# Two gated cross-attention and feed-forward layers: all five engine streams in another order, with the same operations

## The reference

```python
x = x + tanh(g_xattn[0]) * L0_xattn(ctx, ctx, layernorm(x), Wk, Wq, Wv, Wo, biases)   # A
x = x + tanh(g_ffn[0])   * L0_ffn(layernorm(x), w_gate, w_up, w_down)                 # B
x = x + tanh(g_xattn[1]) * L1_xattn(layernorm(x), ctx, Wq, Wkv, Wo)                   # C
x = x + tanh(g_ffn[1])   * L1_ffn(layernorm(x), W, b, lora_down, lora_up, ...)        # D

# A: 16 heads of width 16, the softmax is over the heads
score = einsum('bhij,bhkj->bhik', k, q) / sqrt(16);  attn = softmax(score, axis=1)
# B: h = silu(x @ wg.T) * (x @ wu.T), 768 wide; h @ wd.T
# C: 16 query heads, one key and value head of width 16, softmax over the context rows
# D: a linear layer whose weight has a low-rank addition
```

## Time and profile before

| | |
|---|---|
| median of 3 executions | 2359.47 us (2358.21 to 2359.94) |
| profiled execution | 2358.72 us, its span 2356.9 us |
| mean granted clock of PE | 0.999 of full speed |
| busy share of the span | PE 98%, DVE 93%, POOL 75%, ACT 72% |
| busy share of the 16 DMA engines | 9.9% |
| period of the loop | 35.24 us, 57 iterations |

### The profile page before, as it was taken

How to read it: one execution, slowest core, us unless ns; L and a number is a source line. 1 busy time by engine, 2 the same in 40 slices (tenths; PEclk the granted TensorE clock), 3 DMA queues, 4 the chain that set the end, 5 groups by cost and what they waited for, 6 DMA issues and landing times.

```text
span 2356.9 us, 69621 instructions
## 1 busy us (share of the span) xinstructions
PE 2308.5 (98%) x27827; PEld 2062.3 (87%) x27827; DVE 2200.9 (93%) x3613; ACT 1705.6 (72%) x3402; POOL 1777.8 (75%) x2512
## 2 busy tenths in 40 slices
PE   6999999999999999999999999999999999999998
PEld 5888888889888888888889889889889889889887
DVE  6999999999999999999999999999999999999973
ACT  4667777777777777777777777777777777777664
POOL 3767787787787787787787777777778778778754
PEclk9999999999999999999999999999999999999999
DMA  3000010010010010010010100100100100000000
GB/s 110 28 22 28 29 34 27 29 34 27 29 34 27 29 34 27 29 34 27 31 33 27 34 29 27 34 29 27 34 29 28 33 29 30 31 29 32 20 22 15
DMA packets 74332, 73.33 MB, mean 31 GB/s; under 512 B 6555, under 2 KB 73393, under 8 KB 74290
## 3 DMA queue, kind: packets, MB, share of 16 engines
q1 hardware_dynamic: 74290, 72.75, 9.9%
HBM read 54.90 MB, written 16.78 MB: 30 GB/s over the span
## 4 chain that ended last, share of the span: by engine, by line
PE 56%; DVE 37%; issue 3%; ACT 1%; POOL 1%; DMA 1%; SPq 0%; POOLq 0%; DVEq 0%; ACTq 0%
DVE m L1600 11%; PE work L2383 10%; PE work L2384 9%; PE work L2385 9%; PE scores L2480 6%; PE work L2513 5%; PE work L2500 5%; DVE scores L1597 5%; DVE m L1591 4%; PE work L2420 4%; PE scores L2470 4%; DVE x L1628 4%; PE work L2398 2%; DVE stats_B L1559 2%; DVE stats_D L1559 2%
## 5 line engine op out<-in xcount | busy, mean ns | idle before, releaser
L856 ACT ACTIVATE e<-scores 120x1024 f32<-120x1024 f32 x512 | 517.5, 1042 | 35.9 <-DVE scores L1597 21.5
L2383 PE MATMUL work<-xt_hi_B,w_hi 128*128 128x256 f32 x1536 | 445.0, 290 | 2.8 <-POOL xt_lo_B L426 2.8
L2384 PE MATMUL work<-xt_lo_B,w_hi 128*128 128x256 f32 x1536 | 426.9, 278 | 0.0
L2385 PE MATMUL work<-xt_hi_B,w_lo 128*128 128x256 f32 x1536 | 426.6, 278 | 0.0
L413 POOL TENSOR_TENSOR zt<-e 120x512 f32<-120x512 f32 x256 | 331.1, 1295 | 49.5 <-ACT e L856 40.9
L407 POOL TENSOR_TENSOR h_lo<-h_f,h_hi 128x256 fp32r<-128x256 f32 x384 | 278.9, 740 | 90.5 <-ACT h_hi L803 90.4
L1597 DVE TENSOR_TENSOR scores<-scores,m 120x1024 f32<-120x1024 f32 x256 | 303.0, 1227 | 4.2
L2383 PEld LDWEIGHTS work<-xt_hi_B,w_hi 128*128 128x128 f32 x1536 | 290.8, 189 | 17.0 <-POOL xt_lo_B L426 13.5
L1609 DVE TENSOR_TENSOR e<-e,work 120x2048 f32<-120x2048 f32 x128 | 291.4, 2276 | 0.2
L1591 DVE TENSOR_REDUCE m<-scores 120x128 fp32r<-120x2048 f32 x128 | 290.0, 2266 | 0.9 <-PE scores L2470 0.8
L2384 PEld LDWEIGHTS work<-xt_lo_B,w_hi 128*128 128x128 f32 x1536 | 289.3, 188 | 0.0
(11 more groups left out here) (224 smaller groups left out, 7290.6 us busy)
## 6 DMA issues: line engine op xcount, KB each, us to landing
x_ln<-xp SPq DMA_DIRECT2D x64, 256.0 KB, 2.9
x_res<-xp SPq DMA_DIRECT2D x64, 256.0 KB, 2.8
y<-y_out SPq DMA_DIRECT2D x64, 256.0 KB, 2.2
ctx_f_A<-cp SPq DMA_DIRECT2D x64, 128.0 KB, 2.1
ctx_f_C<-cp SPq DMA_DIRECT2D x64, 128.0 KB, 2.0
qm<-mT SPq DMA_DIRECT2D x256, 4.0 KB
e<-wi SPq DMA_DIRECT2D x3, 768.0 KB, 7.1
w_ctx<-wc SPq DMA_DIRECT2D x1, 656.0 KB
```

The costliest lines, as they stand in the source:

```text
L856: return act.activation(e[0:SC, c, 2 * h:2 * h + 2, :, :].rearrange("p a b n -> p (a b n)"), scores[0:SC, 2 * h:2 * h + 2, :].rearrange("p ...
L2383: pe.matmul(out, a_hi, b_hi_, start=first, stop=False, skip_group_check=parts)
L2384: pe.matmul(out, a_hi, b_lo_, start=False, stop=False, skip_group_check=parts)
L2385: last = pe.matmul(out, a_lo, b_hi_, start=False, stop=end, skip_group_check=parts)
```

## The change

The operations of the loop are the same but for two small copies; their order is another on all five engines.

- **PE.** `rows_out` of D and `gate_up` 0 and 1 stand at the end of an iteration, no longer at its head, which by itself only turns the loop. `scores1(0)` stands between `gate_up` 1 and `gate_up` 2, no longer behind 2. Behind `scores0(1)` come transposes B, `maxima_transposed`, transposes A, `keys0` (before: transposes B, `keys0`, `maxima_transposed`, transposes A). `queries` of C stands ahead of `gate_up` 5. `down(4)` no longer waits for POOL's `hidden_lo(4)`; what it needs is covered by another count.
- **DVE.** `counted` of C and of D are gone (that of B stays). `mean_variance("A")` stands ahead of `reciprocal1`, `low` of A ahead of `mean_variance("D")`, the sums of C ahead of `values0_out`, `mean_variance("C")` between the two `subtract_max` of half 1. `gated` and `hidden` of 0, 1, 3, 4 and the transposed low part of A stand elsewhere.
- **POOL.** One `add_heads` of half 1 is at the iteration's end. The `add_row` into x3_biased stands between `hidden_lo(5)` and `root("D")`; both `add_heads` of half 0 stand between `root("D")` and `root("B")` (before: one was ahead of `hidden_lo(5)`). `last_residual` and `root("C")` stand elsewhere.
- **ACT.** The loop is turned likewise; `ln_apply("B")` stands ahead of the high part of D, the copy into y_out behind `ln_apply("C")`, the exponentials of each pair are swapped.
- **SP.** `load_x_ln` first, then the store, the context for A, the four DMAs of the maxima, `load_x_res` and the context for C. `load_x_res` is now that of t-2.
- **Edges.** The prologue and the epilogue are written anew in the same manner: 283 fillers, 110 and 173. In the first stages 24 stand where 21 did.

```diff
             with nc.tensor.Fori(FIRST + DEPTH, LAST + 1) as t:
-                pe.wait_ge(s["T_out_B"], t - 1)
-                pe.wait_ge(s["T_lo_D"], t)
-                rows_out(W[0], xt_hi["D"], xt_lo["D"], "f1").then_inc(s["f1_mm"], 1)
-                pe.wait_ge(s["T_lo_B"], t)
-                pe.wait_ge(s["mT_out"], t)
-                gate_up(W[3], 0).then_inc(s["G_mm0"], 1)
-                pe.wait_ge(s["kz0_even"], t)
-                gate_up(W[2], 1).then_inc(s["G_mm1"], 1)
-                pe.wait_ge(s["f1_out"], t)
-                gate_up(W[0], 2).then_inc(s["G_mm2"], 1)
                 pe.wait_ge(s["max_rows"], 64 * t)
                 pe.wait_ge(s["A1_exp"], 2 * t + 2)
                 scores1(0).then_inc(s["ends_pe"], 1)
+                pe.wait_ge(s["G_h0"], t)
+                gate_up(W[0], 2).then_inc(s["G_mm2"], 1)
                 pe.wait_ge(s["G_h1"], t)
                 pe.wait_ge(s["ln_C"], t)
                 transposes(W[2], "C").then_inc(s["T_mm_C"], 1)
+                pe.wait_ge(s["f1_out"], t)
                 gate_up(W[3], 4).then_inc(s["G_mm4"], 1)
...
-                gate_up(W[2], 5).then_inc(s["G_mm5"], 1)
                 pe.wait_ge(s["T_lo_C"], t)
                 queries(W[0], "C", "q1").then_inc(s["q_mm_C"], 1)
+                gate_up(W[2], 5).then_inc(s["G_mm5"], 1)
...
-                pe.wait_ge(s["G_lo4"], t)
                 down(W[3], 4)
...
+                pe.wait_ge(s["v0_pad"], t)
+                maxima_transposed(W[0]).then_inc(s["mT_mm"], 1)
+                transposes(W[1], "A").then_inc(s["T_mm_A"], 1)
+                pe.wait_ge(s["q_out_A"], t)
                 pe.wait_ge(s["ld_ctx_A"], 16 * t)
-                pe.wait_ge(s["v0_pad"], t)
                 keys0(W[2]).then_inc(s["k0_mm"], 1)
-                maxima_transposed(W[3]).then_inc(s["mT_mm"], 1)
-                pe.wait_ge(s["q_out_A"], t)
-                transposes(W[1], "A").then_inc(s["T_mm_A"], 1)
+                pe.wait_ge(s["T_lo_D"], t)
+                pe.wait_ge(s["T_out_B"], t)
+                rows_out(W[3], xt_hi["D"], xt_lo["D"], "f1").then_inc(s["ends_pe"], 1)
+                pe.wait_ge(s["T_lo_B"], t)
+                pe.wait_ge(s["mT_out"], t)
+                gate_up(W[0], 0).then_inc(s["G_mm0"], 1)
+                pe.wait_ge(s["kz0_odd"], t)
+                gate_up(W[2], 1).then_inc(s["G_mm1"], 1)
```

More of the change, by code:

```diff
@@ L1176, in _ @@
-            act.wait_ge(s["A1_sub"], 2 * LAST + 4)
-            exponential(e0, 1, 1).then_inc(s["A1_exp"], 1)
+            tanh(0, W[0]).then_inc(s["G_tanh0"], 1)
+            act.wait_ge(s["st_out"], 16 * (LAST + 1))
+            act.activation(y_out[:, :, :], two(W[3], NT), ACT.Copy).then_inc(s["f1_out"], 1)
             act.wait_ge(s["G_mm1"], LAST + 1)
             tanh(1, W[2]).then_inc(s["G_tanh1"], 1)
+            act.wait_ge(s["ends_pe"], 4 * LAST + 5)
+            exponential(e1, 0, 0).then_inc(s["T0_exp"], 1)
@@ L1846, in _ @@
-            hidden(0, W[3]).then_inc(s["G_h0"], 1)
-            normalise(W[1], 0).then_inc(s["A0_p"], 1)
+            hidden(1, W[3]).then_inc(s["G_h1"], 1)
+            hidden(0, W[0]).then_inc(s["G_h0"], 1)
+            dve.wait_ge(s["G_h1"], 8)
+            reciprocal0(W[3], 0).then_inc(s["ends_dve"], 1)
+            dve.wait_ge(s["G_tanh3"], 8)
+            gated(3, W[2]).then_inc(s["G_a3"], 1)
+            dve.wait_ge(s["ends_dve"], 43)
+            normalise(W[3], 0).then_inc(s["A0_p"], 1)
@@ L2066, in _ @@
             dve.wait_ge(s["woC_mm"], LAST + 1)
-            residual(x3, x2_before, W[1]).then_inc(s["res_C"], 1)
+            residual(x3, x2_before, W[2]).then_inc(s["res_C"], 1)
             dve.wait_ge(s["res_C"], LAST + 1)
             sums("D", x3).then_inc(s["ln_mom_D"], 1)
+            dve.wait_ge(s["ln_mom_D"], LAST + 1)
+            counted("D")
+            mean_variance("D").then_inc(s["ln_eps_D"], 1)
+            dve.wait_ge(s["ends_act"], 6 * LAST + 10)
+            low(y_lo["A"][:, :, :], two(W[1], KC), y_hi["A"][:, :, :]).then_inc(s["yA_lo"], 1)
```

2378 lines of the change are left out of this document (1182 added, 1196 removed), and 13 rows, old and new, of the table given.

## The result

The changed kernel takes 2367.16 us (median of 6 runs), the kernel before, in the same session, 2358.84 us (6 runs). The ratio is 1.0035, with a 95% interval of 1.0023 to 1.0048: 8.3 us slower. On another chip the changed kernel took 2371.46 us (5 executions) and the kernel before 2360.81 (9), a ratio of 1.0044 (1.0031 to 1.0058). One of the eleven executions of e9_before_again took 3210.5 us at a granted clock of 0.66; no reading rests on it.

The account below looks back on a forecast made before the run. PE, busy for all but 0.3% of the loop, and DVE, 96%, were taken to hand work to each other in a 35.24 us period. 2358.72 + 3 (PE) - 1 (edges) = 2360.7, rounded to 2361.0 us; range 2351 to 2370.

Parts of the forecast that it names:

- the likeliest outcome, no change: Whole kernel: measured time within 0.2% of the kernel before, 2354.8 to 2364.2 us; chance 0.45.
- a late POOL: POOL's queue from hidden_lo(5) to D's and B's low parts: 0.1 to 0.2 us per iteration, 2366 to 2371; chance 0.28.
- the case that had 0.08, the edges: Loop as forecast, but prologue or epilogue moves by 8 us either way: 2353 or 2369; chance 0.08.
- The first case: Likeliest case, including that nothing moves: 2361 us, own range 2355 to 2366; chance 0.44.
- PE and the loop: PE, gate_up 1 to gate_up 4: 4.37 us instead of 4.30, 0.04 to 0.07 per iteration, taken as +3 us.
- a count of restarts: PE around the moved scores1(0): upper bound of one more matmul restart, 0.11 us per iteration, giving 6 us.
- DVE sheds 0.07 to 0.19 us for nothing: DVE's loop: copy and mean removed ahead of "wo0" or the residual of C, counted as no time gained.
- The second rival: DVE really binds the loop: 0.10 to 0.19 us less per period, 6 to 11 us, put at 2352; chance 0.20.
- POOL just in time: POOL's low part of D ready at 1011.07 for PE's 1011.09; 0.24 us left at B's low part; counted 0.
- the first rival: POOL becomes late for the product of D or gate_up(0): 0.1 to 0.2 us per iteration, 2366 to 2371; chance 0.28.
- gate_up(2) for G_h0, and SP: hidden(0) ends 0.1 to 0.2 us ahead of gate_up(2); SP's DMAs don't delay scores1(0): nothing for SP.
- Edges, -1 ± 4: Prologue and epilogue together: -1 us, with ±4 as a third of the epilogue's idle time.

Follow-up runs that it names:

- e9_before_again: The kernel before once more, unchanged: 2360.22 us, beside 2360.47 us of the kernel before.
- e10_no_counted: The kernel before without DVE's loop copies counted of C and D, low of A and sums of C moved: 2362.58 against 2360.47 us, ratio 1.0008.
- e8_pool_more: The changed kernel with one more half-row-tile addition on POOL between hidden_lo(5) and root D: 2403.96 us, 32.5 more than the changed kernel.
- e6_warm: The changed kernel with more fillers in three prologue gaps, third batch's transposes behind second batch's queries: 2371.84 us beside 2371.46 for the unchanged order.
- e3_last_stage: The changed kernel with the last stage rearranged (exponentials, layer norm, transposes and product of D, parts of C): 2370.66 us, kernel before 2365.14.
- e7_last_fewer: The changed kernel with the last stage rearranged and 14 instead of 32 fillers ahead of the last "wo1": 2370.13 us, kernel before 2360.81.
- e5_after_again: The changed kernel once more, unchanged: 2371.46 us, beside 2360.81 us of the kernel before.

## Why the prediction was right or wrong

The time lies in the range (2351 to 2370), 6 us above the value, and on the side that had a chance of 0.31; the likeliest outcome, no change (0.45), did not occur. That it lies inside is partly luck: the range reached up to 2370 for a late POOL, which did not occur, and the time came in the main from the case that had 0.08, the edges. The first case alone ended at 2366.

- **PE and the loop**: +3 us was forecast, the profile shows 55 x 0.0356 = 2.0 us between the sixth and the 61st batch. The stretch from gate_up 1 to gate_up 4 measured the 4.37 us of the sum, since each piece was a row. But gate_up 4 and 3 behind it took 2.91 us in place of 3.00, and with them nothing is left of the 0.07. What made the loop longer is the pace of other blocks ("wo1" and down 2 and 3, 0.07 us together), less what DVE gave back. So the size is near and the mechanism, a count of restarts, is not what the sum came from; the pace was not in it. That the +3 came out near is luck.
- **DVE sheds 0.07 to 0.19 us for nothing**: wrong by 0.06 us per iteration, 57 x 0.057 = 3.2 us. The prediction took the residual of A to follow "wo0", since it starts 0.10 us behind it; the rows of after show that 0.04 is enough, and that DVE's queue had held it. The second rival's mechanism was there, to a third of the 0.19, and the slower pace took the gain away in the changed kernel and in e10_no_counted alike.
- **POOL just in time**: right, to 0.03 us at the product of D and 0.24 at B's low part, and the first rival did not occur. That it was so near was shown by e8_pool_more. The first rival's argument that a late product of D of up to 0.14 us only eats the wait of gate_up(0) did not hold: the product of D binds first, without that cushion.
- **gate_up(2) for G_h0, and SP**: no wait there; right.
- **Edges, -1 ± 4**: this is the step that failed. Measured +6.6 (3.2 and 3.4 by the residuals of A). It was argued from idle time as something that another order may use, and from the fillers' count, and the clock was no term of it. In the epilogue 0.8 us lie in its first stage, 1.5 in the second and 1.7 in the last, with the rest 0.5 shorter. In the last stage the mis-orders of the product and of the layer norm of D could have been laid on the rows of before. In the prologue the order itself costs little: about 0.7 us up to the first residual, 1.4 in the step 1-2 and 0.6 in 2-3, less 2.4 in 3-6. About 3 us go with PE's clock: 2.0 in the first stage and 1.6 in the step 2-3, less the 0.5 that the kernel before lost in its step 1-2. These are estimates from the second table, and of the falls only those of the first stage were removed by an experiment (e6_warm).

What stays open: 0.8 and 1.5 us in the first two stages of the epilogue, what makes an execution take the slower or the faster pace, and so how much of the loop's difference is order. Seven other profiles with this loop have a mean of 35.31 us, two of before 35.25, which would be 3.6 us. Nor is a profile always like the median: the profiled executions of e3_last_stage and e7_last_fewer took 6 to 7 us less than the medians of their kernels, and that of e5_after_again, near its median, has a period of 35.365. On that chip the loop's share may be 6 of the 10.6 us.

## What to carry to other kernels

In a pipelined loop whose prologue and epilogue are written out, cost the edges block by block like the loop: there each wait counts once, but less work hides it. Fillers that are sized for a gap must be shortened with it, or they become the wait. Before work is moved in the queue of an engine with 25% idle time, count its slack at each consumer; here it was 0.06 us at one and about 0.7 us behind it. A wait of 0.1 us between two engines needs a second look: compare it with the shortest such distance in the trace before you say which of the two was late.

## What the runs showed of the hardware

A matmul of 128 x 256 on the rounded factors follows the last after 0.113 or 0.118 us at a granted clock of 1.00 in the loop. Which of the two holds for a block differs with the order, with the execution and, in some, from one iteration to the next. No row explains it. The period of one loop goes from 35.256 to 35.365 us with it, 6 us in all: one execution of e3_last_stage took 2363.7 us where the ten others took 2369.0 to 2371.6, though that one also had no fall of the clock in the step 2-3.

The wait of PE between the transposes of B and of C was followed by a fall of the granted clock to 0.5 in all but one profile of the changed prologue. In e3_last_stage, with the same waits (0.99 and 1.70 us) as in the changed kernel, the clock stayed at 1.00: a fall is not certain, even for one and the same prologue. Against that step of 29.21 us, profiles with a mean clock of 0.86 from 98 to 110 us took 1.5 to 1.7 us more, and those with 0.72 took 2.1 to 2.3 more.

Between the end of an engine's instruction and the start of what another engine had waiting for it, these traces show 0.04 us from PE to DVE (with PE's ends as the profile models them) and 0.05 from DVE to PE, as means over the loop.
